# A four-layer recurrent block: w2 by chunk of the contraction in four column tiles, d and u folded, dense blocks read a slot later

## The chip, the cores and the metric

One core of a Trainium2 chip runs the kernel. The metric is device time in microseconds (us) of one execution; the host only lays data out.

## The reference

x is 32 sequences of 128 steps of 512 features, cond one row of 512 for each sequence. Four layers follow each other, each added to x:

```python
d = rsqrt(einsum('bi,io->bo', ys * ys, w0 * w0) + EPS)         # ys = cond / sqrt(512)
x1 = x + einsum('bsi,io->bso', x * ys[:, None], w0) * d[:, None]
h = tanh(h @ wh1 + x1_t @ wx1 + b1); x2_t = x1_t + h           # 128 steps, h0 = cond
xw = gelu(layernorm(cond) @ hw1 + hb1) @ hw2 + hb2             # 512 -> 2 * 512 * 8
layer = base + einsum('bdr,bkr->bdk', *halves(xw))             # rank 8, one for each sequence
x3 = x2 + (x2 + einsum('btc,bco->bto', x2, layer))
i, f, o, g = gates(x3_t @ wx3 + b3 + h @ wh3)                  # LSTM, 128 steps, h0 = cond
out_t = x3_t + o * tanh(f * c + i * g)
```

## The kernel before, in words

Time is cut into 32 tiles of 4 steps. Each large product is made in float16 with both operands split into a high and a low part (three products are summed); a scale, a power of two, comes from the largest magnitude of the operand. ScalarE makes the high part (`high`, L444), VectorE the low one (`low`, L625). Largest magnitudes go over the partitions by `partition_all_reduce` on GpSimd (`spread`, L391, for weights; L407 and L425 for tiles of x).

All five engines run lists written out by hand, joined by semaphores. The lists go by slots t = -13 to 127 (`SLOTS`). Slot t holds LSTM step t (from t = 0 on) and the step r of the tanh recurrence (RNN) that `slot_of` puts there: r = t + LEAD in the slots before 0, after that the remaining steps are spread over slots 0 to 117, so some slots (39, 78, 117 and all later ones) have none. a is the LSTM's tile, s = t % 4.

TensorE's slot: `gates_h` (L1120, 48 matmuls in four column tiles) waits for the split LSTM state; `gates_x` of the next step (L1112); `rnn_product` (L1129, L1132); the transpose of the LSTM state (L1175), which waits for VectorE's `lstm_h` (L904); behind it the dense work: by r % 4, halves of `l0` (layer 0's product of tile r//4 + 1) at 0 and 1 and of `l1` (x1 by wx1) at 2 and 3, and by s the layer 2 product `l2` of tile a + 1 (`z` and a quarter of base at s = 0, two quarters at 1, the last and the low rank part at 2). In the slots before t = 0 the w2 pieces of `W2_AFTER` come last.

VectorE's slot: gates out of PSUM (L894), the cell (L897 to L901), `lstm_h`, the RNN sums (L910, L913), the low parts of both states (L919, L928), then the pieces that prepare tiles: at s = 0 `mask_z`, `gate_scales`, `zm_low`; at r % 4 = 1 `x1` (layer 0's result out of PSUM) and `x1_low`; at s = 2 `x3` (layer 2's result); at r % 4 = 3 `tile_scales`, `xs_low` and `xw1` (layer 1's input part out of PSUM); `x2_low` at slots 4a - 5. ScalarE makes the high parts in the same slots. GpSimd adds x2 = x1 + h (L418) each step, ScalarE's tanh of step r waits for that of step r - 1; GpSimd also makes `xs` (x times ys, L399), one tile every four steps, and the partition reduces.

Before the slots lie the loads, the scales and splits of w0, wx1 and wh1, d (L997), the layer norm and u = ae by hw1 (L1004), `l0(0)`, w2 pieces 0 and 1, and `l1(0)`. In the slots before t = 0 also the wx3 and wh3 squares, scales and halves, base, and the layer 2 weights out of w2 are made. A w2 piece is one output chunk: a bias matmul (L1017) and four float32 matmuls (L1021) with 32 columns of weights, all into one column tile of the array; its megabyte comes by one DMA into a ring of four buffers. `copy_rows` moves four finished pieces to SBUF, `move_b` turns b, and after the last piece (t = -1) come `turn_a`, the reduce of a, and layer 2 of tile 0.

SP's list issues all loads in order, with the waits for free buffers between them.

## Time and profile before

| | us |
|---|---|
| median of 3 runs (1312.89 to 1316.41) | 1315.82 |
| the profiled execution | 1317.44 |
| its span, first to last instruction | 1315.4 |
| TensorE busy | 1239.2 (94%) |
| VectorE busy | 795.9 (61%) |
| ScalarE busy | 440.2 (33%) |
| GpSimd busy | 117.7 (9%) |
| TensorE clock granted, mean | 0.982 |

The profile is of one execution. PE is TensorE, PEld its weight loads, DVE VectorE, ACT ScalarE, POOL GpSimd, SP the queue that issues DMAs. Times are us from the first instruction. An instruction's line number is that of the code above; a name stands for a tile without its buffer's number, and several small tiles share storage (x1T, x2 in x_ring, zm and x3T in late). "[1.20 <-DVE lstm_h L904]" behind an instruction is the idle time of its engine before it and what ended it; "issue" is time in which the engine waited for nothing that the profile shows. A float32 matmul leaves two records. The granted clock is a share of 2.4 GHz.

### The profile page before, as it was taken

How to read it: one execution, taken by the hardware profiler on the slowest of the kernel's cores; microseconds unless marked ns; L12 is line 12 of the kernel's file. 1: busy time of each engine (PE TensorE's matmuls, PEld its weight loads, DVE VectorE, ACT ScalarE, POOL GpSimd, SP SyncE). 2: the span in 40 equal slices, each digit the busy share in tenths (PEclk: the TensorE clock that was granted, in tenths of full speed). 3: DMA queues.
4: the chain of work that ended last, by engine and by line, in shares of the span. 5: the costliest groups of instructions: out<-in, count | busy, mean ns of one | idle time of the engine just before them, and what ended most of it. 6: DMA issues, size and time to landing. Idle time of an engine off the chain costs nothing.

```text
span 1315.4 us, 50704 instructions
## 1 busy us (share of the span) xinstructions
PE 1239.2 (94%) x22900; PEld 793.1 (60%) x22900; DVE 795.9 (61%) x2235; ACT 440.2 (33%) x1110; POOL 117.7 (9%) x210
## 2 busy tenths in 40 slices
PE   6949979999999999999999999999999999999997
PEld 5433336666666666666666666666666666666553
DVE  5444546656666666656666666666666666665543
ACT  4253323232332333233333333333333333333322
POOL 2001101001000101000011011100100111000000
PEclk9978889999999999999999999999999999999999
DMA  9832300000000000000000000000000000000000
GB/s 327 335 130 98 112 9 12 17 19 18 19 18 13 17 19 12 17 19 18 19 16 13 19 19 19 19 19 19 18 11 19 19 11 11 11 11 11 10 10 18
DMA packets 22472, 50.99 MB, mean 39 GB/s; under 512 B 1920, under 2 KB 2048, under 8 KB 21232
## 3 DMA queue, kind: packets, MB, share of 16 engines
q1 hardware_dynamic: 22256, 47.75, 10.2%
q8 instruction: 179, 2.93, 0.9%
q14 instruction: 37, 0.30, 0.1%
HBM read 39.36 MB, written 8.39 MB: 36 GB/s over the span
## 4 chain that ended last, share of the span: by engine, by line
PE 73%; DVE 14%; ACT 6%; issue 5%; DMA 1%; SPq 0%; POOL 0%; DVEq 0%; POOLq 0%; ACTq 0%
PE ps_gates L1120 21%; PE ps_gates L1112 19%; PE ps_l L1054 12%; PE ps_x L1054 8%; PE ps_rnn L1129 4%; PE ps_rnn L1132 3%; PE ps_gates L1021 2%; PE ps_lstm_t L1175 2%; PE ps_z L1054 2%; DVE gates_ring L894 1%; ACT gates_ring L525 1%; PE ps_lstm_t L1021 1%; DVE xw1T L721 1%; ACT cell_tanh L530 1%; DVE lstm_h L904 1%
## 5 line engine op out<-in xcount | busy, mean ns | idle before, releaser
L1120 PE MATMUL ps_gates<-big,lstm_h 128*32 128x512 f16 x6144 | 356.7, 381 | 6.0 <-ACT lstm_h L444 6.0
L1112 PE MATMUL ps_gates<-big,rows 128*32 128x512 f16 x6144 | 353.7, 379 | 1.7 <-DVE rows L625 1.7
L1112 PEld LDWEIGHTS ps_gates<-big,rows 128*32 128x32 f16 x6144 | 164.6, 97 | 168.4 <-issue 1.7
L1120 PEld LDWEIGHTS ps_gates<-big,lstm_h 128*32 128x32 f16 x6144 | 153.1, 97 | 159.4 <-ACT lstm_h L444 8.4
L894 DVE SCALAR_TENSOR_TENSOR gates_ring<-ps_gates,tile_un,rows 128x256 f32<-128x256 f32 x256 | 111.9, 479 | 133.5 <-PE ps_gates L1120 133.5
L525 ACT ACTIVATE gates_ring<-gates_ring 128x256 f32<-128x256 f32 x128 | 53.3, 416 | 378.1 <-DVE gates_ring L894 378.1
L418 POOL TENSOR_TENSOR x_ring<-x1T,rnn_h 128x128 f32<-128x128 f32 x128 | 60.8, 475 | 899.2 <-ACT rnn_h L539 681.4
L1129 PEld LDWEIGHTS ps_rnn<-rnn_h,wh_hi 128*128 128x128 f16 x2048 | 90.8, 97 | 66.7 <-issue 56.4
L1129 PE MATMUL ps_rnn<-rnn_h,wh_hi 128*128 128x64 f16 x2048 | 121.3, 192 | 9.7 <-DVE rnn_h L928 9.7
L1132 PE MATMUL ps_rnn<-rnn_h,wh_lo 128*128 128x32 f16 x2048 | 116.5, 177 | 0.0
L928 DVE SCALAR_TENSOR_TENSOR rnn_h<-rnn_h,scales 128x128 f16<-128x128 f32 x128 | 76.3, 596 | 42.2 <-ACT rnn_h L444 39.5
L910 DVE SCALAR_TENSOR_TENSOR rnn_half<-ps_rnn,un_rnn,xw1T 128x128 f32<-128x128 f32 x128 | 44.8, 350 | 91.1 <-PE ps_rnn L1132 90.6
L444 ACT ACTIVATE lstm_h<-ps_lstm_t,tile_g 128x128 f16<-128x128 f32 x128 | 47.1, 368 | 149.0 <-PE ps_lstm_t L1175 149.0
L1132 PEld LDWEIGHTS ps_rnn<-rnn_h,wh_lo 128*128 128x128 f16 x2048 | 91.7, 97 | 0.0
L1054 PE MATMUL ps_l<-xs,w_hi 128*128 128x128 f16 x1024 | 81.5, 225 | 8.2 <-DVE xs L625 8.2
L1054 PE MATMUL ps_l<-x,wx_hi 128*128 128x128 f16 x1024 | 79.4, 221 | 6.9 <-DVE x L625 6.9
L1054 PE MATMUL ps_x<-x,base_hi 128*128 128x128 f16 x1024 | 79.4, 221 | 2.6 <-DVE base_lo L625 2.6
L1054 PEld LDWEIGHTS ps_l<-xs,w_hi 128*128 128x128 f16 x1024 | 68.8, 102 | 8.9 <-DVE xs L625 6.3
L904 DVE TENSOR_TENSOR lstm_h<-gates_ring,cell_tanh 128x128 f32<-128x128 f32 x128 | 38.3, 299 | 57.6 <-ACT cell_tanh L530 57.6
L1054 PEld LDWEIGHTS ps_l<-x,wx_hi 128*128 128x128 f16 x1024 | 67.5, 101 | 8.6 <-DVE x L625 7.2
L530 ACT ACTIVATE cell_tanh<-cell 128x128 f32<-128x128 f32 x128 | 39.6, 309 | 88.2 <-DVE cell L901 88.2
L897 DVE TENSOR_TENSOR late<-gates_ring,cell 128x128 f32<-128x128 f32 x128 | 37.5, 293 | 48.1 <-ACT gates_ring L527 48.1
(185 smaller groups left out, 1616.3 us busy)
## 6 DMA issues: line engine op xcount, KB each, us to landing
ring<-in_hw SPq DMA_DIRECT2D x16, 1024.0 KB, 7.2
xT_sb<-in_xT SPq DMA_DIRECT2D x32, 256.0 KB, 2.8
outT<-late SPq DMA_DIRECT2D x32, 256.0 KB, 2.0
big<-in_wx SPq DMA_DIRECT2D x5, 1024.0 KB, 9.8
big<-in_wh SPq DMA_DIRECT2D x5, 1024.0 KB, 18.5
big<-in_w SPq DMA_DIRECT2D x1, 1024.0 KB, 5.6
big<-in_hw SPq DMA_DIRECT2D x1, 1024.0 KB, 12.4
late<-in_base SPq DMA_DIRECT2D x1, 1024.0 KB, 15.4
```

Source lines behind the costliest of these rows:

```text
L418: nc.gpsimd.tensor_tensor(x2T[i % X2_RING][:, :, s], x1T[i % 2][:, :, s], rnn_h[:], ALU.add)\
L444: return nc.scalar.activation(out_, in_, ACT.Copy, scale=scale)
L525: nc.scalar.activation(gates[:, 0:2 * P], gates[:, 0:2 * P], ACT.Sigmoid).then_inc(gates_acted, 1)
L530: nc.scalar.activation(cell_tanh[:], cell[:], ACT.Tanh).then_inc(cell_tanh_ready, 1)
L894: nc.vector.scalar_tensor_tensor(gates[:, half], ps_gates[t % 2][:, half], tile_un[:, a, 0:1], b3_sb[:, half], ALU.mult, ALU.add).then_inc ...
L904: nc.vector.tensor_tensor(lstm_h[:], gates[:, 2 * P:3 * P], cell_tanh[:], ALU.mult)\
L928: nc.vector.scalar_tensor_tensor(rnn_h16[:, :, 1], rnn_h[:], s_h, rnn_h16[:, :, 0], ALU.mult, ALU.subtract).then_inc(rnn_lo_ready, 1)
L1054: last = nc.tensor.matmul(psum, w, x, start=(first and n == 0), stop=(final and n == len(triples) - 1))
L1112: nc.tensor.matmul(ps_gates[t % 2][B * j:B * j + B, :], x16[:, part, k, at:at + B], wx3_part(w_part, k)[:, GW * j:GW * j + GW], start=(n = ...
L1120: last = nc.tensor.matmul(ps_gates[t % 2][B * j:B * j + B, :], lstm_h16[:, part, k], wh3_part(w_part, k)[:, GW * j:GW * j + GW], start=Fal ...
L1129: nc.tensor.matmul(ps_rnn[:, at:at + 2 * B], wh1_hi[:, k, P * oc:P * oc + P], rnn_h16[:, k].rearrange("p h b -> p (h b)"), start=(k == 0), ...
L1132: last = nc.tensor.matmul(ps_rnn[:, at:at + B], wh1_lo[:, k, P * oc:P * oc + P], rnn_h16[:, k, 0], start=False, stop=(k == KC - 1))
```

## The change

- w2 comes by chunk of the contraction: a megabyte of the ring now holds, for one of four chunks k, four output chunks j. `w2_unit` multiplies them in four column tiles side by side; the four biases come with k = 0. Sixteen units, as there were sixteen pieces.
- d and u are made in four column tiles (`folded_parts`), copied to SBUF by VectorE, and the four parts are added by matmuls with a stack of identities, `fold` (`unfolded`).
- The weight scales come one by one, as do the reduces behind them; tile 0's scale comes before those of tiles 1 to 3. hw1 is loaded before wh1, base later.
- LEAD is 14. `slot_of` then leaves slots 29, 58, 88, 117 and later ones without an RNN step.
- `l0`'s halves are made at r % 4 = 3 (for the tile after) and 0, and read (`x1`) at 1; `l1`'s at 2 and 3, and `xw1` stands at the next 0, before the RNN sums. Layer 2 of a tile is made at s = 3, 0 and 1, `x2_low` at slots 4a - 6; `mask_z` and `x3` keep their slots. `xs_low` moves to 2, `tile_scales` to 0, `x_magnitude` and its reduce to 3, GpSimd's `xs` to 1.
- The squares of wx3 and wh3, their halves, base's preparation, `copy_rows` and `move_b` shift by about a slot.

```diff
-LEAD = 13
+LEAD = 14
...
             def load_w2(n):
-                sp.dma_start(ring[:, n % RING].rearrange("p (k n) -> p k n", k=KC),
-                             hw2[1 - n // RANK, n % RANK].rearrange(by_chunk, p=P)).then_inc(ld_ring[n % RING], 16)
+                q, k = n // KC, n % KC
+                sp.dma_start(ring[:, n % RING].rearrange("p (j n) -> p j n", j=RH),
+                             hw2[1 - q // 2, RH * (q % 2):RH * (q % 2 + 1), P * k:P * k + P].rearrange("j p n -> p j n"))\
+                  .then_inc(ld_ring[n % RING], 16)
...
             load_weight(wx1, WX1_SLOT, ld_wx1)
+            load_weight(hw1, W1_SLOT, ld_w1)
             load_weight(wh1, WH1_SLOT, ld_wh1)
-            load_weight(hw1, W1_SLOT, ld_w1)
...
-            for n in range(RING + 2, 2 * RANK):
+            for n in range(RING + 1, 4 * KC):
                 sp.wait_ge(w2_used, n - RING + 1)
                 load_w2(n)
+                if n == RING + 1:
+                    sp.dma_start(late[:].rearrange("p (k n) -> p k n", k=KC), base.rearrange(by_chunk, p=P)).then_inc(ld_base, 16)
...
             xs(0)
+            pool.wait_ge(sq_ready, 1)
+            pool.wait_ge(cond_max_ready, 1)
+            spread(slice(0, 2))
+            pool.wait_ge(m_ready, 1)
+            spread_x(0, 1)
+            pool.wait_ge(sq_ready, 2)
+            spread(slice(2, 3))
             pool.wait_ge(sq_ready, 3)
-            pool.wait_ge(cond_max_ready, 1)
-            spread(slice(0, 4))
+            spread(slice(3, 4))
             pool.wait_ge(m_ready, XT_RING)
-            nc.gpsimd.partition_all_reduce(m_all[:], m_part[:], P, MAX).then_inc(m_spread, XT_RING)
+            spread_x(1, XT_RING - 1)
             xs(1)
...
-                    if s == 2 and i + 2 < TILES:
+                    if s == 1 and i + 2 < TILES:
                         xs(i + 2)
-                    if s == 2 and XT_RING <= i + 3 < TILES:
+                    if s == 3 and XT_RING <= i + 3 < TILES:
                         pool.wait_ge(m_ready, i + 4)
                         wait(pool, tile_s_ready, i + 3)
-                        nc.gpsimd.partition_all_reduce(m_all[:, 0:1], m_part[:, 0:1], P, MAX).then_inc(m_spread, 1)
-                    if r == 2:
+                        spread_x(0, 1)
+                    if r == 3:
                         pool.wait_ge(sq_ready, 7)
-                        pool.wait_ge(base_max_ready, 1)
-                        spread(slice(7, 12))
+                        spread(slice(8, 12))
                     if r == 6:
                         pool.wait_ge(sq_ready, 11)
                         spread(slice(12, 16))
-                    if r == 9:
+                    if r == 10:
+                        pool.wait_ge(base_max_ready, 1)
                         pool.wait_ge(b_max_ready, 1)
                         spread(slice(4, 6))
+                        spread(slice(7, 8))
...
+            act.wait_ge(w_scale_ready, 1)
+            high(flat(w0_hi), big[:, W0_SLOT], s_w0).then_inc(w_hi_ready, 1)
+            act.wait_ge(d_var_ready, 1)
+            nc.scalar.activation(root_d, var_d, ACT.Sqrt).then_inc(d_root_ready, 1)
+            xs_high(0)
+            act.wait_ge(w_scale_ready, 2)
+            high(flat(wx1_hi), big[:, WX1_SLOT], s_wx1).then_inc(w_hi_ready, 1)
             act.wait_ge(ld_wh1, 16)
             act.wait_ge(sq_ready, 2)
             squares(unused16, big[:, WH1_SLOT], 3)
-            act.wait_ge(d_var_ready, 1)
-            nc.scalar.activation(root_d, var_d, ACT.Sqrt).then_inc(d_root_ready, 1)
-            act.wait_ge(scales_ready, 1)
-            high(flat(w0_hi), big[:, W0_SLOT], s_w0).then_inc(w_hi_ready, 1)
...
             nc.scalar.activation(hyperT, hyperT, ACT.Gelu).then_inc(hyper_ready, 1)
+            x1_high(0)
+            act.wait_ge(w_scale_ready, 3)
             high(flat(wh1_hi), big[:, WH1_SLOT], s_wh1).then_inc(w_hi_ready, 1)
+            act.wait_ge(h_scale_ready, 1)
             high(rnn_h16[:, :, 0], condT_sb[:], s_h).then_inc(h0_hi, 1)
-            x1_high(0)
-            act.wait_ge(xs_lo_ready, 1)
             xs_high(1)
...
+            WX3_SQUARED = {1: (0,), 2: (1, 2), 3: (3,)}
+            WH3_SQUARED = {4: (0,), 5: (1, 2), 6: (3,)}
...
-                if r is not None and r < KC:
-                    wx3_squares(r)
-                if r is not None and 3 <= r < 3 + KC:
-                    wx3_high(r - 3)
+                if r is not None and r in WX3_SQUARED:
+                    for k in WX3_SQUARED[r]:
+                        wx3_squares(k)
                 if r is not None and 4 <= r < 4 + KC:
-                    wh3_squares(r - 4)
-                if r == 7:
-                    copy_rows(1)
+                    wx3_high(r - 4)
...
-                if r is not None:
-                    c = r // STEPS + 1
-                    if r % STEPS == 1 and c < TILES:
-                        x1_high(c)
-                    if r % STEPS == 3 and c + 1 < TILES:
-                        wait(act, l0_ps, c + 1)
-                        xs_high(c + 1)
+                    x3_high(a + 1)
+                if t in x2_split and t != -1:
+                    x2_high(x2_split[t])
+                if r is not None and r % STEPS == 2 and r // STEPS + 2 < TILES:
+                    xs_high(r // STEPS + 2)
...
+
+            def weight_scale(n):
+                dve.wait_ge(absmax_spread, n)
+                col = slice(n, n + 1)
+                linked(nc.vector.tensor_scalar(exps[:, col], absmax_all[:, col], LEAST ** 2, None, ALU.max))
+                linked(exponents(exps[:, col], exps[:, col]))
+                half_exponents(exps[:, col])
+                over_power(scales[:, col], exps[:, col], TOP).then_inc(w_scale_ready, 1)
...
+            weight_scale(1)
+            linked(nc.vector.tensor_scalar(exps[:, 7:8], absmax_all[:, 0:1], 1.0, None, ALU.max))
+            linked(exponents(exps[:, 7:8], exps[:, 7:8]))
+            over_power(scales[:, 7:8], exps[:, 7:8], TOP).then_inc(h_scale_ready, 1)
+            dve.wait_ge(h_scale_ready, 1)
+            linked(nc.vector.tensor_scalar(m_shift[:, 0:1], s_h, 2.0 ** -(TOP - 3), None, ALU.mult))
+            dve.wait_ge(dsum_parts, 1)
+            nc.vector.tensor_copy(folded, ps_x3[:]).then_inc(dsum_moved, 1)
+            tile_scales(0, 1, 0)
+            dve.wait_ge(dsum_ready, 1)
+            nc.vector.tensor_scalar(var_d, ps_rnn[:, 0:P].rearrange("p (k b) -> p k b", b=B), L0_EPS, None, ALU.add)\
+              .then_inc(d_var_ready, 1)
+            weight_scale(2)
+            dve.wait_ge(w_scale_ready, 2)
+            tile_undo(0, 1, 0)
+            dve.wait_ge(u_parts, 1)
+            nc.vector.tensor_copy(folded, ps_z[:]).then_inc(u_moved, 1)
...
+            weight_scale(3)
+            dve.wait_ge(w_scale_ready, 3)
+            linked(nc.vector.tensor_tensor(un_rnn[:], s_wh1, s_h, ALU.mult))
+            linked(over_power(un_rnn[:], un_rnn[:], 0))
...
-            linked(over_power(un_rnn[:], un_rnn[:], 0))
+            for c in range(1, XT_RING):
+                x_magnitude(c, c)
+            tile_scales(1, XT_RING - 1, 1)
+            tile_undo(1, XT_RING - 1, 1)
             xs_low(1)
             dve.wait_ge(ld_b1, 16)
-            xw1(0)
...
                 if r is not None:
+                    if r % STEPS == 0:
+                        xw1(r // STEPS)
+                        dve.wait_ge(xw1_ready, r // STEPS + 1)
                     dve.wait_ge(rnn_ps, r + 1)
-                    dve.wait_ge(xw1_ready, r // STEPS + 1)
...
-                    if r == 1:
-                        linked(base_rows(0))
-                    if r == 2:
-                        base_magnitude()
-                    if r == 3:
+                    if r == 4:
                         wx3_scale()
...
-                    if r == 8:
-                        b_magnitude()
-                    if r == 10:
-                        b_bounds()
+                    if 5 <= r < 5 + KC:
+                        wx3_low(r - 5, 1)
                     if 9 <= r < 9 + KC:
                         wh3_low(r - 9, 1)
+                    if r == 8:
+                        base_diagonal()
+                        linked(base_rows(0))
+                    if r == 9:
+                        base_magnitude()
+                    if r == 10:
+                        b_magnitude()
+                    if r == 12:
+                        b_bounds()
+                c, ahead = (-1, -1) if r is None else (r // STEPS + 1, r % STEPS)
...
+                if ahead == 1 and c < TILES:
+                    x1(c)
...
-                        x1(c)
-                    if r % STEPS == 2 and XT_RING <= c + 2 < TILES:
-                        dve.wait_ge(m_spread, c + 2)
-                        x_magnitude(c + 2, 0)
+                if ahead == 3 and XT_RING <= c + 2 < TILES:
+                    x_magnitude(c + 2, 0)
+                if ahead == 0 and XT_RING <= c + 1 < TILES:
+                    tile_scales(c + 1, 1, 0)
+                    tile_undo(c + 1, 1, 0)
+                if ahead == 1 and c < TILES:
+                    x1_low(c)
...
-                if r is not None:
-                    c = r // STEPS + 1
-                    if r % STEPS == 1 and c < TILES:
-                        x1_low(c)
-                    if r % STEPS == 3:
-                        if XT_RING <= c + 2 < TILES:
-                            tile_scales(c + 2, 1)
-                        if c + 1 < TILES:
-                            xs_low(c + 1)
-                        if c < TILES:
-                            xw1(c)
+                if t in x2_split and t != -1:
+                    x2_low(x2_split[t])
+                if ahead == 2 and c + 1 < TILES:
+                    xs_low(c + 1)
...
+            def folded_parts(psum, xT_, w):
+                for k in range(KC):
+                    last = nc.tensor.matmul(psum[B * k:B * k + B, :], xT_[:, k], w[:, k], start=True, stop=True,
+                                            tile_position=(0, B * k))
+                return last
+
+
+            def unfolded(psum):
+                for k in range(KC):
+                    last = nc.tensor.matmul(psum[:, B * k:B * k + B], folded[:, P * k:P * k + P], fold[:], start=True, stop=True)
+                return last
+
             pe.wait_ge(ys_ready, 2)
             pe.wait_ge(sq_ready, 1)
-            for oc in range(KC):
-                for k in range(KC):
-                    last = nc.tensor.matmul(ps_x3[:, B * oc:B * oc + B], w0_sq[:, k, P * oc:P * oc + P], ysq[:, k],
-                                            start=(k == 0), stop=(k == KC - 1))
-            last.then_inc(dsum_ready, 1)
+            folded_parts(ps_x3, ysq, w0_sq).then_inc(dsum_parts, 1)
+            pe.wait_ge(dsum_moved, 1)
+            unfolded(ps_rnn).then_inc(dsum_ready, 1)
...
+            def w2_unit(n):
+                q, k = n // KC, n % KC
                 if n == 0:
                     pe.wait_ge(hyper_ready, 1)
                     pe.wait_ge(ld_b2, 16)
-                if n == 2 * RH:
+                if n == 2 * KC:
                     pe.wait_ge(rows_ready, 1)
-
-                at = RANK * (1 - q // 2) + RH * (q % 2) + j
-                nc.tensor.matmul(ps_rows[q][B * j:B * j + B, :], ident[0:2 * RANK, at:at + 1].broadcast_to([2 * RANK, B]), b2_sb,
-                                 start=True, stop=False, tile_position=(0, B * j))
+                if k == 0:
+
+                    for j in range(RH):
+                        at = RANK * (1 - q // 2) + RH * (q % 2) + j
+                        nc.tensor.matmul(ps_rows[q][B * j:B * j + B, :], ident[0:2 * RANK, at:at + 1].broadcast_to([2 * RANK, B]),
+                                         b2_sb, start=True, stop=False, tile_position=(0, B * j))
                 pe.wait_ge(ld_ring[n % RING], 16 * (n // RING + 1))
-                for k in range(KC):
-                    last = nc.tensor.matmul(ps_rows[q][B * j:B * j + B, :], hyperT[:, k], ring[:, n % RING, D * k:D * k + D],
+                for j in range(RH):
+                    last = nc.tensor.matmul(ps_rows[q][B * j:B * j + B, :], hyperT[:, k], ring[:, n % RING, D * j:D * j + D],
                                             start=False, stop=(k == KC - 1), tile_position=(0, B * j))
                 last.then_inc(w2_used, 1)
...
-            W2_AFTER = {0: (2, 3), 1: (4,), 3: (5,), 6: (6,), 7: (7,), 8: (8, 9), 9: (10,), 10: (11,), 11: (12, 13), 12: (14, 15)}
...
-            def l2(a, s):
-                if s == 0:
+            def l2(t):
+                s = t % STEPS
+                a = (t + 5) // STEPS
+                if a < TILES and (s == 3 or t == 0):
                     z(a)
                     wait(pe, x3_ready, a)
                     x3_base((0,))
-                if s == 1:
+                if a < TILES and s == 0:
                     x3_base((1, 2))
-                if s == 2:
+                if a < TILES and s == 1:
                     x3_base((3,))
                     x3_low_rank(a)
...
-            w2_piece(1)
+            w2_unit(0)
...
                 if r is not None:
-                    c = r // STEPS + 1
-                    if c < TILES:
-                        if r % STEPS == 0:
-                            l0(c, (0, 1))
-                        if r % STEPS == 1:
-                            l0(c, (2, 3)).then_inc(l0_ps, 1)
-                        if r % STEPS == 2:
-                            l1(c, (0, 1))
-                        if r % STEPS == 3:
-                            l1(c, (2, 3)).then_inc(xw1_ps, 1)
-                    if t >= 0 and a + 1 < TILES:
-                        l2(a + 1, s)
+                    c, ahead = r // STEPS + 1, r % STEPS
+                    if ahead == 0 and c < TILES:
+                        l0(c, range(KC) if c == 1 else (2, 3)).then_inc(l0_ps, 1)
+                    if ahead == 2 and c < TILES:
+                        l1(c, (0, 1))
+                    if ahead == 3 and c < TILES:
+                        l1(c, (2, 3)).then_inc(xw1_ps, 1)
+                    if ahead == 3 and c + 1 < TILES:
+                        l0(c + 1, (0, 1))
+                    if t >= 0:
+                        l2(t)
```

## Rows read from the trace of the kernel before

**Rows 1.** Stages: busy us (x instructions) of PE, PEld, DVE, ACT, POOL; clock; DMA.
```profile
45.00:176.00 131.00, 107.00 (x861) 48.05 (x857) 59.42 (x122) 47.92 (x63) 14.84 (x22) 0.87 0.40 151
...
920.00:1228.00 308.00, 308.00 (x6232) 204.90 (x6224) 197.69 (x575) 105.33 (x290) 27.27 (x49) 1.00 0.04 13
```

**Rows 2.** Waits of TensorE, 195 to 1316 us: total, times, longest.
```profile
PE ps_lstm_t L1175 <- DVE lstm_h L904: 22.0, 29, 2.9
PE ps_gates L1120 <- ACT lstm_h L444: 6.0, 13, 0.5
```

**Rows 3.** Timeline of TensorE: start, us, instruction, idle before and releaser.
```profile
198.60 0.31 PE L1175 MATMUL ps_lstm_t<-ident,lstm_h 128*128 128x128 f32 x1
...
201.55 2.77 PE L1120 MATMUL ps_gates<-big,lstm_h 128*32 128x512 f16 x48
...
208.23 0.33 PE L1175 MATMUL ps_lstm_t<-ident,lstm_h 128*128 128x128 f32 x1 [0.35 <-DVE lstm_h L904]
...
227.82 0.33 PE L1175 MATMUL ps_lstm_t<-ident,lstm_h 128*128 128x128 f32 x1 [1.20 <-DVE lstm_h L904]
...
560.82 0.33 PE L1175 MATMUL ps_lstm_t<-ident,lstm_h 128*128 128x128 f32 x1 [2.17 <-DVE lstm_h L904]
561.60 4.46 PE L1120 MATMUL ps_gates<-big,lstm_h 128*32 128x512 f16 x48 [0.46 <-ACT lstm_h L444]
```

**Rows 4.** Timeline of VectorE: h0_lo, r = 7, t = -1, t = 0.
```profile
37.87 0.35 DVE L625 SCALAR_TENSOR_TENSOR rnn_h<-condT_sb,scales,rnn_h 128x128 f16<-128x128 f32 x1
...
117.72 0.15 DVE L681 TENSOR_TENSOR m_exp<-m_all,m_least 128x3 f32<-128x3 f32 x1
...
118.91 0.75 DVE L625 SCALAR_TENSOR_TENSOR xs<-xsT,tile_s,xs 128x512 f16<-128x512 f32 x1
...
188.94 0.75 DVE L625 SCALAR_TENSOR_TENSOR rows<-ps_x,tile_un,rows 128x512 f16<-128x512 f32 x1 [3.98 <-ACT rows L444]
...
190.27 0.74 DVE L625 SCALAR_TENSOR_TENSOR x<-x_ring,tile_s,x 128x512 f16<-128x512 f32 x1
...
200.34 0.35 DVE L928 SCALAR_TENSOR_TENSOR rnn_h<-rnn_h,scales 128x128 f16<-128x128 f32 x1 [0.36 <-ACT rnn_h L444]
200.99 0.29 DVE L832 TENSOR_TENSOR late<-ps_z,same_b 128x128 f32<-128x128 f32 x1 [0.30 <-PE ps_z L1054]
...
202.18 0.28 DVE L705 TENSOR_SCALAR d_un<-dT,tile_s 128x128 f32<-128x128 f32 x1
...
204.70 0.75 DVE L625 SCALAR_TENSOR_TENSOR x<-x1T,tile_s,x 128x512 f16<-128x512 f32 x1 [0.79 <-ACT x L444]
```

**Rows 5.** Timeline of TensorE in the start: d, a w2 piece, b.
```profile
10.75 7.01 PE L997 MATMUL ps_x<-added,big 128*128 128x32 f32 x32 [1.02 <-ACT big L450]
...
51.03 1.04 PE L1017 MATMUL ps_gates<-x_ring,ident 16*32 16x512 f32 x2
52.00 3.62 PE L1021 MATMUL ps_gates<-ring,lstm_h 128*32 128x512 f32 x8
...
137.04 1.08 PE L1032 MATMUL ps_x<-rows,half_ident 128*64 128x512 f32 x4
```

**Rows 6.** Waits of GpSimd, whole span.
```profile
POOL x_ring L418 <- issue: 217.9, 30, 8.9
POOL m_all L425 <- issue: 166.4, 28, 6.3
```

**Rows 7.** Timeline of GpSimd.
```profile
175.66 0.38 POOL L391 PARTITION_ALL_REDUCE absmax_all<-absmax  x1 [10.20 <-DVE absmax L628]
```

**Rows 8.** Timeline of ScalarE.
```profile
46.13 0.31 ACT L539 ACTIVATE rnn_h<-rnn_pre 128x128 f32<-128x128 f32 x1 [10.61 <-DVE rnn_pre L913]
...
82.88 0.31 ACT L539 ACTIVATE rnn_h<-rnn_pre 128x128 f32<-128x128 f32 x1 [5.65 <-POOL x_ring L418]
...
105.79 1.89 ACT L450 ACTIVATE gates_ring<-big 128x2048 f16<-128x2048 f32 x1
```

**Rows 9.** Granted clock around slot 39, columns as in rows 1.
```profile
558.00:566.00 8.00, 5.37 (x65) 2.12 (x61) 3.21 (x10) 2.19 (x6) 0.10 (x1) 0.79 0.10 35
```

186 lines of the change are left out of this document (88 added, 98 removed).

## The prediction, made before the run

> **What bounds the kernel now.** I read the stage table first [rows 1]. From 45 to 176 us, the start in which the tanh recurrence runs alone, TensorE is busy for 107 of 131 us, and the granted clock is 0.87. In the main stage it has no gap at all in the third quarter (308.00 of 308). So the start can be shortened, and the main stage can hardly be: what is left there are stalls. The waits of TensorE after 195 us sum to 28.0 us [rows 2]; all are waits for the LSTM cell on VectorE (L904) or for its split (L444). The timeline shows their pattern [rows 3]: while tile boundary and RNN phase stand as they do before t = 39, two slots of each four stall the transpose L1175, by 0.35 us and by 1.20 us (ten and nine times); at t = 39, a slot without RNN step, the stall is 2.17 us, 0.46 us follow, and the next L1120 group takes 4.46 us in place of 2.77. That is 3.5 + 10.9 + 2.2 + 0.5 + 1.7 = 18.8 us, and some 1.4 us of single waits until t = 117: 20.2 us in all. The remaining 9.7 us lie in the last eleven slots, which the change leaves alone.
>
> **The rule of a stall.** VectorE comes late to the gates where its work at the end of a slot is longer than TensorE's. In slot 0 the transpose starts at 198.60 and the last piece on VectorE ends at 204.70 + 0.67 = 205.37, 6.77 us later; behind the transpose TensorE has 2.71 us of dense work D; the stall is 0.35 [rows 3, 4]. So stall = x - D - 3.71, with x the end of VectorE's work after the transpose. RNN split done is at x = 2.1 (200.34 + 0.35 - 198.60), so with E the work behind it, stall = E - D - 1.61. With D = 0, L1120 starts 0.78 us after the transpose (561.60 - 560.82) where otherwise D + 0.24 (201.55 - 198.60) pass: D counts as 0.54, and 0.5 us are lost at L1120 besides.
>
> **Main stage, added.** Prices [rows 4]: mask_z and gate_scales 1.0 with zm_low 1.2 (200.99 to 202.18), x1 1.75 and then 0.79 of waiting for ScalarE's half and 0.67 for x1_low (202.18 to 205.37), x3 1.33 (188.94 to 190.27), x2_low 0.67, xs_low 0.67, tile_scales with tile_undo 1.2 (117.72 to 118.91). xw1 now stands before the RNN sums, in time that VectorE has free once the cell is done: nothing, unless VectorE is late already. Moving l0, l1 and L2 a slot ahead removes VectorE's waits for TensorE. What stays is how the pieces meet, and slot_of sets that: with LEAD 14 the gaps are at t = 29, 58, 88, 117, and r % 4 = 0 falls on t % 4 = 2, 3, 0 and 1 in the four stretches between.
> First stretch, seven periods: s = 2 has E = 1.2 + 1.33 + 0.67 = 3.2 against D = 1.34, s = 3 has E = 3.2 against 1.38: 0.44 a period, 3.1 us.
> Second, seven: s = 0 carries mask, x1 and x1_low, 1.0 + 1.75 + 0.79 + 0.67 = 4.2, against D = 1.34: 1.24 each, 8.7 us.
> Third, seven: 0.24 each, 1.7 us.
> Fourth, from t = 90, six times: r % 4 = 1 meets s = 2. E = 1.75 + 0.79 + 0.67 + 1.33 + 0.67 = 5.2, and TensorE has nothing behind the transpose, since the list gives no l0 or l1 at r % 4 = 1 and no L2 at s = 2. Stall 5.2 - 0.54 - 1.61 = 3.1, with the 0.5 at L1120 3.6: 21.8 us, and 0.5 at t = 114.
> Gaps: 1.8 us together, mostly the 0.46 at L1120.
> Sum 37.6 us against 20.2: +17.4.
> **Moved out.** One RNN product (0.86 us) and half an l0 (1.34 us) go from the main stage to the start: -2.2.
> **Clock.** The 2.17 us stall was followed by a stretch at 1.2 in place of 2.4 GHz: 0.79 of the clock granted over 558 to 566 us [rows 9], 1.7 us lost in L1120. Six stalls of 3.1 us could cost 0 to 10.2 us; since one event in mid-kernel carries the price, I take the middle, 5.
>
> **The start, removed.** A w2 piece costs 3.55 + 0.97 us [rows 5], sixteen 72.3. A unit puts four column tiles side by side; the two half-width tiles of b show that float32 products overlap so, four records in 1.08 us where a lone pair takes 1.04. Sixteen units at 0.9 and four biases at 1.0 make 18.4: 53.9 us less on TensorE. The d and u products drop from 7.01 each to about 1.8 of parts, 0.74 of copy and 1.75 of folding, but on VectorE the copies and scales now stand ahead of weight_low(0), so I count no gain there. Behind it ScalarE's square of wh1 (2.1) and weight_scale(3) (1.0) have moved ahead of wh1's halves, with 0.3 of hand-over: h0_lo, which ended at 38.2 [rows 4], ends near 41.6.
> **The start, what takes its place: GpSimd.** Every time it goes from ordinary work to a partition reduce, 5.94 us pass (166.4 / 28), and back to ordinary work 7.26 (217.9 / 30) [rows 6], with nothing that the profile shows: a pair costs 5.94 + 0.38 + 7.26 = 13.6 us. ScalarE's tanh of step r waits for the x2 sum of step r - 1; the 5.65 us at 82.88 are such a wait [rows 8]. Before, pairs lie behind r = 2, 6 and 9, 10; after, behind r = 3, 6, 7, 10 and 11. Moreover x_magnitude(1 to 3) moved behind h0_lo, so the reduce over tiles 1 to 3 comes at 43.5 and xs(1) only after the way back:
> - 41.6 + 1.9 (magnitudes) + 0.4 + 7.3 + 1.3 (xs) + 1.4 (halves) + 0.9 (xw1) + 0.8: tanh of r = 0 at 55.6, before 46.13 [rows 8].
> - r = 1 to 3 hold x1(1), four squares of 2.1 (1.89 and a read) on ScalarE [rows 8], and xs_high: about 20, so the sum of r = 3 at 75.8.
> - pair: 89.4. Steps 5 and 6 with wx3 halves and wh3 squares, 12.8: 102.2.
> - two pairs and a sum, 27.6: 129.9. Steps 9 and 10, 9.6: 139.5.
> - two pairs, two reduces, a sum, 28.0: 167.5. Step 13 1.4, and 5.9 to the reduce of a: 174.8.
> Before, that reduce is at 175.66 [rows 7]; what follows it is the same. Gain 0.9 us. Bounds: if no pair were waited for, ScalarE and VectorE alone give some 25 us less; if DMA or the split of r = 0 slip, 8 us more.
> DMA: w2 moves the same bytes in the same sizes; a ring load has a slot or more, which GpSimd now stretches: nothing. If short slots came back, unit 13 or 14 would wait for its megabyte, some us.
>
> **Sum.** +17.4 - 2.2 + 5.0 - 0.9 = +19.3. The profiled execution took 1317.44 us (span 1315.4), 1.6 above the median 1315.82: 1336.7 there, 1335 as a median.
>
> **Rivals.**
> A, faster: GpSimd's changes aren't waited for (only a first use of a kind is dear, or the change overlaps with the wait for its operand). Then the 54 us count as far as VectorE and ScalarE let them: -25 + 17.4 - 2.2 = -9.8, 1306, down to 1296 with smaller stalls. It decides from about 17 us of gain in the start. For it: 53.9 us leave the busiest engine. Against it: the 58 changes of rows 6 average 5.9 and 7.3 us. 0.18. The Trainium skill, GPSIMD Engine Reference, section Instruction dispatch, puts a load of about 6 us on the first call to a freshly loaded kernel: read as once a kernel's life, it gives A's time; by rows 6 the 5.94 agrees in size, but comes at each change of kind.
> B, faster: the start as I have it, but the stalls of the last stretch are hidden: -0.9 - 2.2 + 17.4 - 21.8 = -7.5, 1308. Against it is D = 0 there. 0.07.
> C, slower still: the late r = 0 and ScalarE's squares push every pair, +8, and full clock loss, +5: 1348. 0.1.
> D, the tiles don't overlap in float32: units cost what pieces cost, slots from r = 8 grow as before; about 1341. Rows 5 speak against it. 0.02.
> Forecast 0.55; of the 0.08 left half is slower, half no change. Of A and B 0.03 end within 0.3% (4 us, about what a measurement of this kernel can tell from no change). So slower 0.55 + 0.12 + 0.04 = 0.71, same 0.07, faster 0.22. Low 1304 takes in most of A and B, high 1347 the sum at full clock loss and part of C.
>
> **What would show it.** Right: ScalarE waits for GpSimd at the tanh of r = 5, 9 and 13; VectorE waits for ScalarE's xs half at 44 to 54; L1175 stalls about 3 us every fourth slot from t = 91, and 1.2 in the second stretch; w2 groups of some 0.9 us. Wrong: gates of t = 0 ending before 185 us (195.0 now), or a last stretch without stalls.

## The result, and the profile after

| | before | after |
|---|---|---|
| median of the runs, us | 1315.59 (4 runs) | 1377.27 (4 runs, 1374.46 to 1382.52) |
| span of the profiled execution | 1315.4 | 1375.6 |
| gates of t = 0 begin on VectorE | 195.25 | 208.00 |
| last LSTM cell: `lstm_h` of t = 127 begins | 1311.21 | 1371.44 |
| TensorE busy | 1239.2 (94%) | 1192.1 (87%) |
| TensorE clock granted, mean | 0.982 | 0.955 |

The changed kernel takes 1.0477 times as long (95% interval 1.0442 to 1.0512), 61.7 us more. The forecast had the sign, but its 1335 was 42 us too low and its range ended at 1347. Of the 60.2 us between the spans, 12.8 lie before the gates of t = 0 and 47.5 between them and the last cell.

The stages of the changed kernel (columns as in rows 1):

```profile
45.00:176.00 131.00, 60.71 (x896) 41.77 (x896) 61.72 (x130) 48.49 (x63) 14.58 (x23) 0.72 0.44 167
920.00:1228.00 308.00, 283.81 (x5524) 184.48 (x5513) 180.96 (x522) 93.92 (x259) 26.62 (x46) 0.97 0.04 14
```

TensorE is busy for 60.71 of 131 us in the start, where it was busy for 107.00 [rows 1]: 46 us of its work have gone, and still the gates of t = 0 begin 12.8 us later. The granted clock of the stage is 0.72 in place of 0.87. From 920 to 1228 it now idles for 24 us; before it had no gap there. TensorE's waits from 195 us on, answering to rows 2:

```profile
PE ps_lstm_t L1240 <- DVE lstm_h L961: 37.5, 36, 2.9
PE ps_gates L1177 <- DVE rows L661: 21.9, 7, 3.6
PE ps_gates L1185 <- ACT lstm_h L469: 9.2, 20, 0.5
```

The waits at the transpose (22.0 before) and at `gates_h` (6.0) have grown, and a new one has appeared: `gates_x` (L1177) waits for x3's low half, `rows`, for 21.9 us in seven waits. One of these, 1.7 us, lies ahead of the gates of t = 0 and is there before too; the other six are in the last stretch.

**The main stage.** The timeline of TensorE (start, us, instruction, idle before) shows one stall of the second stretch, one of the third, and the pair that comes with each tile of the last:

```profile
513.69 0.33 PE L1240 MATMUL ps_lstm_t<-ident,lstm_h 128*128 128x128 f32 x1 [2.21 <-DVE lstm_h L961]
...
784.92 0.33 PE L1240 MATMUL ps_lstm_t<-ident,lstm_h 128*128 128x128 f32 x1 [1.21 <-DVE lstm_h L961]
...
1039.35 2.77 PE L1185 MATMUL ps_gates<-big,lstm_h 128*32 128x512 f16 x48 [0.46 <-ACT lstm_h L469]
1045.66 4.46 PE L1177 MATMUL ps_gates<-big,rows 128*32 128x512 f16 x48 [3.54 <-DVE rows L661]
```

The four stretches have periods (four slots, from one such stall to the next) of 36.5, 37.5, 36.5 and 41.1 us; less their stalls the second and third leave 35.3. In the last, 0.46 at `gates_h` and 3.54 at `gates_x` are lost, and the 48 matmuls behind the long wait take 4.46 us instead of 2.77. The granted clock of that stretch (columns as in rows 1) is 0.61, and it was 1.00 in the 3.60 us before:

```profile
1045.60:1050.00 4.40, 4.34 (x48) 1.64 (x48) 3.19 (x9) 1.21 (x4) 0.00 (x0) 0.61 0.01 3
```

The timeline of VectorE in that slot:

```profile
1040.32 1.45 DVE L987 SCALAR_TENSOR_TENSOR rnn_h<-rnn_h,scales 128x128 f16<-128x128 f32 x1 [0.35 <-ACT rnn_h L469]
1041.69 0.27 DVE L752 TENSOR_SCALAR d_un<-dT,tile_s 128x128 f32<-128x128 f32 x1
...
1044.20 0.75 DVE L661 SCALAR_TENSOR_TENSOR x<-x1T,tile_s,x 128x512 f16<-128x512 f32 x1 [0.79 <-ACT x L469]
1044.87 0.74 DVE L661 SCALAR_TENSOR_TENSOR rows<-ps_x,tile_un,rows 128x512 f16<-128x512 f32 x1
...
1046.19 0.74 DVE L661 SCALAR_TENSOR_TENSOR x<-x_ring,tile_s,x 128x512 f16<-128x512 f32 x1
1046.85 0.87 DVE L951 SCALAR_TENSOR_TENSOR gates_ring<-ps_gates,tile_un,rows 128x256 f32<-128x256 f32 x2
```

and of GpSimd:

```profile
1039.93 0.45 POOL L442 TENSOR_TENSOR x_ring<-x1T,rnn_h 128x128 f32<-128x128 f32 x1 [8.59 <-ACT rnn_h L587]
1040.34 1.28 POOL L417 TENSOR_TENSOR xsT<-xT_sb,ysT 128x512 f32<-128x512 f32 x1
```

The RNN's low half (L987) takes 1.45 us, where the same instruction took 0.35 in rows 4 at 200.34. It starts 0.02 us before GpSimd's 1.28 us of `xs`, and ends 0.15 us after it. From t = 0 on 26 of its 114 executions are that long, one in each tile that has an `xs`. The kernel before had them too, at r % 4 = 2; VectorE and GpSimd there:

```profile
209.63 1.44 DVE L928 SCALAR_TENSOR_TENSOR rnn_h<-rnn_h,scales 128x128 f16<-128x128 f32 x1
...
209.66 1.27 POOL L399 TENSOR_TENSOR xsT<-xT_sb,ysT 128x512 f32<-128x512 f32 x1
```

There VectorE then waited 2.33 us for the next gates, so the 1.1 us cost nothing. In the changed kernel's slot no such time is left: behind L987 stand x1 (from 1041.69), the wait for its high half, x1_low (1044.20), x3's low half (1044.87, for which `gates_x` waits) and x2_low (1046.19); the next gates begin at 1046.85.

**The start.** The timeline of ScalarE, tanh of r = 0, 5, 9 and 13:

```profile
60.93 0.31 ACT L587 ACTIVATE rnn_h<-rnn_pre 128x128 f32<-128x128 f32 x1 [2.32 <-DVE rnn_pre L972]
...
96.32 0.31 ACT L587 ACTIVATE rnn_h<-rnn_pre 128x128 f32<-128x128 f32 x1 [2.62 <-POOL x_ring L442]
...
140.15 0.31 ACT L587 ACTIVATE rnn_h<-rnn_pre 128x128 f32<-128x128 f32 x1 [11.22 <-POOL x_ring L442]
...
179.70 0.31 ACT L587 ACTIVATE rnn_h<-rnn_pre 128x128 f32<-128x128 f32 x1 [12.75 <-POOL x_ring L442]
```

and that of GpSimd: the reduce of tiles 1 to 3 and `xs` of tile 1, the pair behind r = 3, the second of the two pairs behind r = 6 and 7, and the reduce of a:

```profile
44.86 0.37 POOL L410 PARTITION_ALL_REDUCE m_all<-m_part  x1 [15.19 <-DVE m_part L668]
56.55 1.25 POOL L417 TENSOR_TENSOR xsT<-xT_sb,ysT 128x512 f32<-128x512 f32 x1 [11.32 <-issue]
...
88.26 0.39 POOL L405 PARTITION_ALL_REDUCE absmax_all<-absmax  x1 [6.71 <-issue]
95.79 0.44 POOL L442 TENSOR_TENSOR x_ring<-x1T,rnn_h 128x128 f32<-128x128 f32 x1 [7.14 <-issue]
...
131.73 0.38 POOL L410 PARTITION_ALL_REDUCE m_all<-m_part  x1 [7.88 <-issue]
139.62 0.44 POOL L442 TENSOR_TENSOR x_ring<-x1T,rnn_h 128x128 f32<-128x128 f32 x1 [7.51 <-issue]
...
187.77 0.38 POOL L405 PARTITION_ALL_REDUCE absmax_all<-absmax  x1 [6.01 <-issue]
```

Tanh of r = 0 comes at 60.93 (46.13 before [rows 8]), the reduce of a at 187.77 (175.66 before [rows 7]). The way back from the reduce at 44.86 to `xs` of tile 1 takes 11.32 us, in which TensorE does nothing, and behind it `l0` runs at half speed (1.03 us for eight matmuls, 0.61 at full clock). The timeline of TensorE shows that, and two w2 units, as cheap as was thought:

```profile
59.52 1.03 PE L1117 MATMUL ps_l<-xs,w_hi 128*128 128x128 f16 x8 [15.03 <-DVE xs L661]
...
64.12 1.93 PE L1084 MATMUL ps_gates<-ring,lstm_h 128*32 128x512 f32 x16
```

1.93 us for two units, 0.96 each (a lone one takes 1.06 to 1.08), where the matmuls of a piece took 3.62 [rows 5].

### The profile page after: what moved, and what is told of

Read it like the earlier page. It is cut to its first block, busy times and chain, and to the rows that moved or that the text cites. A ratio compares the mean times of both kernels' runs of the same rounds, so it can differ in the third digit from the quotient of the medians.

```text
span 1375.6 us, 50564 instructions
## 1 busy us (share of the span) xinstructions
PE 1192.1 (87%) x22868; PEld 778.9 (57%) x22868; DVE 793.7 (58%) x2252; ACT 436.9 (32%) x1110; POOL 118.3 (9%) x219
## 4 chain that ended last, share of the span: by engine, by line
PE 63%; DVE 17%; issue 11%; ACT 8%; DMA 1%; POOL 0%; SPq 0%; DVEq 0%; POOLq 0%; ACTq 0%
PE ps_gates L1185 18%; PE ps_gates L1177 18%; PE ps_l L1117 10%; PE ps_x L1117 6%; PE ps_rnn L1194 4%; PE ps_rnn L1197 2%; ACT x L469 2%; DVE x1T L759 2%; DVE x1T L755 2%; PE ps_lstm_t L1240 1%; DVE gates_ring L951 1%; PE ps_z L1117 1%; DVE rnn_h L987 1%; ACT rnn_h L469 1%; ACT gates_ring L573 1%
## 5 line engine op out<-in xcount | busy, mean ns | idle before, releaser
L1177 PE MATMUL ps_gates<-big,rows 128*32 128x512 f16 x6144 | 363.5, 387 | 21.9 <-DVE rows L661 21.9
L1177 PEld LDWEIGHTS ps_gates<-big,rows 128*32 128x32 f16 x6144 | 166.7, 98 | 196.6 <-DVE rows L661 24.7
L987 DVE SCALAR_TENSOR_TENSOR rnn_h<-rnn_h,scales 128x128 f16<-128x128 f32 x128 | 78.2, 611 | 54.5 <-ACT rnn_h L469 52.1
L1117 PEld LDWEIGHTS ps_l<-x,wx_hi 128*128 128x128 f16 x1024 | 68.7, 102 | 15.6 <-DVE x L661 13.6
L1240 PE MATMUL ps_lstm_t<-ident,lstm_h 128*128 128x128 f32 x128 | 40.1, 313 | 37.6 <-DVE lstm_h L961 37.5
## 6 DMA issues: line engine op xcount, KB each, us to landing
big<-in_hw SPq DMA_DIRECT2D x1, 1024.0 KB, 10.2
```

The source lines that it names most:

```text
L987: nc.vector.scalar_tensor_tensor(rnn_h16[:, :, 1], rnn_h[:], s_h, rnn_h16[:, :, 0], ALU.mult, ALU.subtract).then_inc(rnn_lo_ready, 1)
L1117: last = nc.tensor.matmul(psum, w, x, start=(first and n == 0), stop=(final and n == len(triples) - 1))
L1177: nc.tensor.matmul(ps_gates[t % 2][B * j:B * j + B, :], x16[:, part, k, at:at + B], wx3_part(w_part, k)[:, GW * j:GW * j + GW], start=(n = ...
L1240: nc.tensor.transpose(ps_lstm_t[:, 0:P], lstm_h[:], ident[:]).then_inc(lstm_t_ps, 1)
```

## The experiments

Thirteen kernels. The kernel before was timed again beside each group of them, at 1312.2 to 1315.0 us; the ratios given are to that time, and differences between kernels of different groups carry some 2 us of it. Line numbers in an experiment's rows are those of its own text, a few lines off from the changed kernel's where an edit takes lines out.

### The w2 units alone, on the kernel before

```diff
-                q, j = n // RH, n % RH
+                q, k = n // KC, n % KC
...
-                for k in range(KC):
-                    last = nc.tensor.matmul(ps_rows[q][B * j:B * j + B, :], hyperT[:, k], ring[:, n % RING, D * k:D * k + D],
+                for j in range(RH):
+                    last = nc.tensor.matmul(ps_rows[q][B * j:B * j + B, :], hyperT[:, k], ring[:, n % RING, D * j:D * j + D],
```

with the loads and the biases as in the change, and all else as before.

> The kernel before with w2 by chunk in four column tiles alone: 53.9 us of TensorE leave the start, nothing else moves. Theory G (GpSimd's changes between ordinary work and reduces set the start once TensorE doesn't): before, only the tanh of r = 4 and r = 8 waits for GpSimd, the other slots for TensorE; those shorten to about the 8 to 9 us of ScalarE's and VectorE's work, and two pairs of changes behind r = 6 and 9, 10 become the bound: 20 to 32 us less, 1284 to 1296. Rival T (TensorE's time is what the start costs, whoever else works): 45 us or more less, below 1272. Rival N (the gain was hidden anyway): within 5 us of 1315.

Measured: 1300.02 us, 0.989 of before (0.9861 to 0.9918). The gates of t = 0 begin at 177.76 instead of 195.25, and from there to the last cell it takes 1116.6 us (before 1116.0). This part of the change gives 14 to 17 us. The time lies 4 us above the range that theory G gave (1284 to 1296) and far from both rivals; T is refuted: some of the 54 us of TensorE's work were on the path, the rest stood beside ScalarE, VectorE and GpSimd.

### The changed kernel with the old w2 pieces

```diff
-                q, k = n // KC, n % KC
+                q, j = n // RH, n % RH
```

with the loads and matmuls of w2 as before, and all else as in the change.

> The changed kernel with w2 in pieces again, one column tile each, as before; everything else as changed. Theory G: the slots behind r = 3, 6, 7, 10 and 11 wait 13 to 15 us for GpSimd whatever TensorE does, so the 54 us of TensorE that come back lie mostly beside those waits: 2 to 12 us slower than the changed kernel (1379 to 1389). Rival T: 35 us or more slower.

Measured: 1390.24 us, 1.0581 (1.0555 to 1.0607), 13 us above the changed kernel and 1 us past the end of G's range; gates of t = 0 at 218.79, 10.8 us later, and the main stage as long as before (1163.6). The units are worth 11 to 13 us here too, and theory T falls for the second time. So the 61.7 us are a loss of some 75 by the other parts, less this gain.

### GpSimd's `xs` in another slot

```diff
-                    if s == 1 and i + 2 < TILES:
+                    if s == 0 and i + 2 < TILES:
                         xs(i + 2)
```

> The changed kernel with GpSimd's product xs at r % 4 = 0 in place of 1, one character. Theory P (VectorE's low part of the RNN state, L987, takes 1.45 us in place of 0.35 where GpSimd makes its sum and xs back to back, and that slot is the one that holds x1): the 1.45 moves to the slot of r % 4 = 0 or is spread there, stalls of the transpose fall from 0.85, 2.21 and 1.21 us to about 0, 1.2 and 0.2, and the last stretch loses 1.1 of 5.7 us a period: 20 to 30 us faster than the changed kernel, 1347 to 1357. Rival V (the 1.1 us too much in each stretch come from VectorE's own order, xw1 before the sums): no change of the stalls, within 4 us of 1377.

Measured: 1343.11 us, 1.0217 (1.0201 to 1.0234), 34 us below the changed kernel, more than expected; 30.5 of it from the first gates on and 3.6 ahead of them (of these 3.6 it isn't shown that they belong to the edit: three kernels with the same start, the changed one and two further down, have these gates at 205.42 to 208.00). VectorE's low half at L987 is back at 0.35 us, in all tiles of the main stage but one:

```profile
550.69 0.35 DVE L987 SCALAR_TENSOR_TENSOR rnn_h<-rnn_h,scales 128x128 f16<-128x128 f32 x1 [0.36 <-ACT rnn_h L469]
```

and GpSimd's `xs` runs elsewhere, behind a change of kind:

```profile
563.66 0.45 POOL L442 TENSOR_TENSOR x_ring<-x1T,rnn_h 128x128 f32<-128x128 f32 x1 [6.80 <-issue]
564.08 1.27 POOL L417 TENSOR_TENSOR xsT<-xT_sb,ysT 128x512 f32<-128x512 f32 x1
```

The stalls fall by 1.1 us in three stretches: 2.21 to 1.12 in the second, 1.21 to none in the third, 3.54 to 2.45 at `gates_x` in the last. In the first the 0.86 us of one slot vanish. That the instruction is slowed by GpSimd's `xs` beside it is shown by this run and by its converse further down (four edits).

### One recurrent step in every slot

```diff
-RNN_SPREAD = 118
+RNN_SPREAD = 114
```

> The changed kernel with RNN_SPREAD 114 in place of 118: no slot without an RNN step until 114, so r % 4 = 0 stays on t % 4 = 2 and the second, third and fourth stretch never come; the number of slots with and without RNN is the same. Theory S (what the main stage loses is set by how r % 4 and t % 4 meet): all 28 periods take 36.5 us as in the first stretch, none 37.5 or 41.1, no stall at gates_x but that of t = -1: 23 to 33 us faster than the changed kernel, 1344 to 1354. Rival O (the order of pieces costs its time in any phase, or the lone slots cost it): within 8 us of 1377.

Measured: 1342.09 us, 1.0208 (1.0190 to 1.0226), 35 us below the changed kernel. Nearly all periods are 36.5 us (the longest 36.9), and `gates_x` waits nowhere in the main stage. Theory S holds: the last stretch's cost is that x1 and x3 share a slot.

### x3 ahead of x1 where both share a slot

```diff
+                if t >= 0 and s == 2 and a + 1 < TILES:
+                    x3(a + 1)
                 if ahead == 1 and c < TILES:
                     x1(c)
...
                     x1_low(c)
-                if t >= 0 and s == 2 and a + 1 < TILES:
-                    x3(a + 1)
```

and x3's high part ahead of x1's on ScalarE.

> The changed kernel with x3 (both engines' parts) ahead of x1 and x1's halves in a slot that holds both. Theory X (in the last stretch gates_x waits 3.5 us for x3's low half because x1, the wait for its high half and its low half stand ahead of it on VectorE, and one half-clock stretch of 1.7 us follows): the six periods of the last stretch take 36.5 to 37.5 us instead of 41.1, the other stretches stay, time 1348 to 1358. Rival Z (x3 itself is ready too late, since z and the low-rank product come late on TensorE): the wait at gates_x stays above 2 us and the time above 1368.

Measured: 1384.04 us, 1.0528 (1.0504 to 1.0552), 7 us above the changed kernel (its interval ends at 1.0512), and as much from the first gates to the last cell. Both expectations failed: X in all, Z in the wait that it kept. The wait at `gates_x` is gone (0.36), but the transpose of the next slot waits as long:

```profile
1045.28 2.77 PE L1177 MATMUL ps_gates<-big,rows 128*32 128x512 f16 x48 [0.36 <-DVE rows L661]
...
1052.51 0.47 PE L1240 MATMUL ps_lstm_t<-ident,lstm_h 128*128 128x128 f32 x1 [3.49 <-DVE lstm_h L961]
```

The period of the last stretch is 41.3 us, against 41.1, and in the first stretch, where x3's slot had a stall of 0.2 to 0.5 us, it now has 0.5 to 1.0. So the order within the slot doesn't help: VectorE has more work in it than the slot holds, and TensorE waits for the rest at one place or at the other.

### Two pairs of changes fewer in the start

```diff
-                if ahead == 3 and XT_RING <= c + 2 < TILES:
+                if ahead == 2 and XT_RING <= c + 2 < TILES:
                     x_magnitude(c + 2, 0)
...
-                    if s == 3 and XT_RING <= i + 3 < TILES:
+                    if s == 2 and XT_RING <= i + 3 < TILES:
```

The first is VectorE's, the second GpSimd's.

> The changed kernel with the magnitude of the later x tiles, and its reduction on GpSimd, one slot earlier, so that in the start they stand right behind the reductions at r = 6 and r = 10 and two of the five pairs of changes of kind are gone. Theory G (in the start the path runs through GpSimd's changes of kind; the waits of tanh at r = 9 and r = 13, 11.2 and 12.8 us, are those of the two pairs that follow each other): both waits fall under 4 us, the reduction of a comes 12 to 24 us earlier (164 to 176 instead of 187.8), main loop unchanged within 4 us, time 1353 to 1366. Rival L (the start is held by the loads, the squares and the rounding of wx3 and wh3, GpSimd only stands beside it): the reduction of a comes less than 6 us earlier, time at least 1371.

Measured: 1362.72 us, 1.0368 (1.0342 to 1.0394), 14.6 us below the changed kernel; the reduce of a at 172.06, 15.7 us earlier, main loop 1163.0 us (1163.4 without the edit). GpSimd's timeline in this run:

```profile
117.62 0.38 POOL L410 PARTITION_ALL_REDUCE m_all<-m_part  x1 [5.71 <-issue]
117.92 0.90 POOL L405 PARTITION_ALL_REDUCE absmax_all<-absmax  x1
```

and ScalarE's tanh of r = 9 and 13:

```profile
133.04 0.31 ACT L587 ACTIVATE rnn_h<-rnn_pre 128x128 f32<-128x128 f32 x1 [1.97 <-DVE rnn_pre L972]
...
164.33 0.31 ACT L587 ACTIVATE rnn_h<-rnn_pre 128x128 f32<-128x128 f32 x1 [3.96 <-DVE rnn_pre L972]
```

The two reduces stand back to back, with nothing between them, and neither tanh waits for GpSimd any more. Theory G holds: a change of kind (GpSimd going from ordinary work to a reduce or back) is paid for each change, not for each reduce.

### The magnitudes of tiles 1 to 3 early

```diff
+            pool.wait_ge(m_ready, XT_RING)
+            spread_x(1, XT_RING - 1)
             pool.wait_ge(sq_ready, 3)
             spread(slice(3, 4))
-            pool.wait_ge(m_ready, XT_RING)
-            spread_x(1, XT_RING - 1)
...
+            for c in range(1, XT_RING):
+                x_magnitude(c, c)
             weight_low(0, w0_lo, w0_hi, W0_SLOT, s_w0)
...
-            for c in range(1, XT_RING):
-                x_magnitude(c, c)
```

> The changed kernel with the magnitudes of x tiles 1 to 3 taken on VectorE ahead of the low half of w0 and reduced on GpSimd ahead of the last weight column, so that the product ysT times x of tile 1 follows the third reduction instead of the fourth. Theory E (the first recurrent step waits 12 to 15 us for the change back to tensor_tensor behind the late reduction at 44.86): tanh of r = 0 comes at 46 to 52 us instead of 60.9, reduction of a 8 to 14 us earlier, time 1362 to 1369. Rival W (the next thing is late as well: w2 units, wx3 loads, so the gain is eaten by the rest of the start): tanh of r = 0 comes early but the reduction of a by under 4 us, time at least 1372.

Measured: 1367.15 us, 1.0398 (1.0367 to 1.0428), 10.1 us below the changed kernel. Tanh of r = 0 comes at 49.66, 11.3 us earlier; the gates of t = 0 8.1 us earlier. GpSimd's timeline at the last early reduce and `xs` of tile 1:

```profile
31.02 0.74 POOL L405 PARTITION_ALL_REDUCE absmax_all<-absmax  x1
38.44 1.26 POOL L417 TENSOR_TENSOR xsT<-xT_sb,ysT 128x512 f32<-128x512 f32 x1 [6.68 <-DVE x1T L759]
```

Theory E holds.

### The two edits of the main stage together

```diff
-RNN_SPREAD = 118
+RNN_SPREAD = 114
...
-                    if s == 1 and i + 2 < TILES:
+                    if s == 0 and i + 2 < TILES:
```

> The changed kernel with both earlier edits, ysT times x in the slots of r mod 4 = 0 and a spread of 114 (one recurrent step in each slot until they end). Each alone gave 34 to 35 us. Theory P plus S (two separate causes, VectorE's slowed instruction beside GpSimd in all stretches and the phase at which x1 and x3 meet in the last): periods of 35.4 to 35.8 everywhere, time 1306 to 1318. Rival O (one and the same cause, both edits only move x1 away from x3): time 1334 to 1345.

Measured: 1321.90 us, 1.0059 (1.0036 to 1.0081). That is 4 us above the range of P plus S, and 12 below that of O. Added, the gains would be 69 us; they are 55: some 10 are counted twice in the second, third and last stretch, by their periods, and 4 ahead of the first gates. From the first gates to the last cell it takes 1110.0 us, in place of 1163.4: 53.5 of the changed kernel's main stage are these two causes, and what is left is 6 us shorter than before.

### d's and u's products as before

```diff
-            folded_parts(ps_x3, ysq, w0_sq).then_inc(dsum_parts, 1)
-            pe.wait_ge(dsum_moved, 1)
-            unfolded(ps_rnn).then_inc(dsum_ready, 1)
+            product(ps_rnn, ysq, w0_sq).then_inc(dsum_ready, 1)
```

`product` is the loop of four by four matmuls of before; u likewise, and VectorE's two copies go.

> The changed kernel with d's and u's products as before (sixteen matmuls each, no parts, no copy, no folding). Theory N (the fold gains nothing: TensorE has nothing else to do there, and VectorE's two copies and two waits, some 3 us, stand ahead of everything that follows): the low half of xs of tile 0 ends 2 to 4 us before 29.4, time 1370 to 1377. Rival F (the fold is what makes the start of the changed kernel as early as it is): time 1380 to 1387, 5 us per product later.

Measured: 1373.88 us, 1.0442 (1.0414 to 1.0470), 3.4 us below the changed kernel, and the gates of t = 0 3.7 us earlier. The intervals overlap, so the traces have to decide. TensorE's timeline of this run, d's and u's products:

```profile
10.79 7.01 PE L1044 MATMUL ps_rnn<-added,big 128*128 128x32 f32 x32 [1.06 <-ACT big L475]
17.61 7.01 PE L1044 MATMUL ps_l<-cell_tanh,big 128*128 128x32 f32 x32
```

VectorE's, the low half of tile 0's xs:

```profile
25.23 0.74 DVE L661 SCALAR_TENSOR_TENSOR xs<-xsT,tile_s,xs 128x512 f16<-128x512 f32 x1
```

The changed kernel's, `unfolded` of d on TensorE:

```profile
21.94 1.91 PE L1054 MATMUL ps_rnn<-fold,x1T 128*128 128x32 f32 x8 [9.05 <-DVE x1T L730]
```

and the same low half on VectorE:

```profile
28.72 0.74 DVE L661 SCALAR_TENSOR_TENSOR xs<-xsT,tile_s,xs 128x512 f16<-128x512 f32 x1
```

The two products take 7.01 us each but are done at 24.6; folded, d's takes 1.93 and 1.91 us and waits 9.05 between them for VectorE's copy. The low half comes 3.5 us earlier without the fold, and tanh of r = 0 at 56.91, where it lies at 59.78 to 62.43 in the seven kernels that have the fold and late magnitudes. In time the fold costs about 3 to 4 us: 3.4 here, 4.4 in the pair of kernels in the next section, whose intervals don't overlap. Theory N holds.

### Four edits, five edits

Early magnitudes, later magnitudes a slot earlier, `xs` at r % 4 = 0 and the spread of 114:

> The changed kernel with all four edits: magnitudes of x tiles 1 to 3 early, later magnitudes one slot earlier, ysT times x in slots of r mod 4 = 0, spread 114. If the four causes are separate, the gains add: 1321.9 less 10.1 (early) less 14.5 (later magnitudes) = 1297, expected 1290 to 1303, faster than before by 1 to 1.8 per cent. If the two edits of the start overlap (the waits that one takes away are those that the other shortens), 1304 to 1312. The run says nothing for the change as made; it asks whether the causes found account for the loss.

and with d and u as before on top:

> The same, and d's and u's products as before. Theory N: 1 to 4 us below the run with the four edits. Rival F: 3 to 10 us above it. The faster of the two is to be compared with the kernel before that had the w2 units alone, 1300.0.

Measured: 1316.33 us, 1.0008 (0.9994 to 1.0022), and 1311.96 us, 0.9978 (0.9964 to 0.9993). The first is 19 us above the expected 1297 and outside both ranges; the second is 4.4 us below the first, 0.4 more than theory N allowed. The start gave all it should (gates of t = 0 at 178.97 and 178.75), but the main loop takes 1129.7 and 1129.2 us instead of 1110.0. The first of the two, GpSimd:

```profile
204.67 0.45 POOL L442 TENSOR_TENSOR x_ring<-x1T,rnn_h 128x128 f32<-128x128 f32 x1 [6.70 <-ACT rnn_h L587]
205.08 1.29 POOL L417 TENSOR_TENSOR xsT<-xT_sb,ysT 128x512 f32<-128x512 f32 x1
```

VectorE in the same slot:

```profile
205.06 1.46 DVE L987 SCALAR_TENSOR_TENSOR rnn_h<-rnn_h,scales 128x128 f16<-128x128 f32 x1 [0.36 <-ACT rnn_h L469]
```

TensorE in the next:

```profile
208.44 2.77 PE L1177 MATMUL ps_gates<-big,rows 128*32 128x512 f16 x48 [0.83 <-DVE rows L661]
```

and GpSimd in the run with the two edits of the main stage:

```profile
592.62 0.44 POOL L442 TENSOR_TENSOR x_ring<-x1T,rnn_h 128x128 f32<-128x128 f32 x1 [7.05 <-issue]
593.04 1.73 POOL L417 TENSOR_TENSOR xsT<-xT_sb,ysT 128x512 f32<-128x512 f32 x1
```

There the reduce at r % 4 = 3 held GpSimd for 7.05 us of changing back, so that the sum and `xs` of the next slot came late, behind L987. With the reduce a slot earlier GpSimd is ready in time, `xs` starts beside L987 again, which takes 1.46 us, and x3 behind it comes 0.83 us late for `gates_x`. From t = 0 on L987 is slow in 26 tiles here and in none of the run with the two edits. Saving a pair of changes in the start brought the slowed instruction back in the main loop.

### The later magnitudes earlier in the start only

On top of the five edits:

```diff
-                if ahead == 2 and XT_RING <= c + 2 < TILES:
+                if ahead == (2 if t < 0 else 3) and XT_RING <= c + 2 < TILES:
```

and likewise on GpSimd.

> As the run with five edits (1312.0), but the later magnitudes are one slot earlier only while the recurrence runs alone (t below 0), and where they were from t = 0 on. Theory M (the magnitude in the slots r mod 4 = 2, where x3 and x2's low half stand at this spread, is what made the main loop 19 us longer, 1128 us against 1109 from the first gates to the last cell, by 0.8 us at gates_x and 0.3 at the transpose in each period): the start stays (gates of t = 0 at 180), the main loop takes 1107 to 1112 us, time 1291 to 1297, below the kernel before with the w2 units alone (1300.0). Rival R (an earlier start shifts something else, a load or the end of the recurrence): main loop above 1120, time 1303 to 1312.

Measured: 1291.78 us, 0.9842 (0.9827 to 0.9857), gates of t = 0 at 177.66, main loop 1108.8 us. The time is the one expected; the reason that theory M gave was half right. The edit is the right one, but at this spread x3 shares its slot with r % 4 = 0 and not with the magnitude; by the rows above, read later, it is the reduce's place on GpSimd that counts, and here the low half of the RNN state is slow in no tile of the main loop. This is the fastest version, 1.6% below the kernel before. It is 0.5% below the units alone by the ratios (0.984 against 0.989; the intervals, up to 0.9857 and from 0.9861, just don't overlap).

### The flat spread on the kernel before

```diff
-RNN_SPREAD = 118
+RNN_SPREAD = 115
```

> The kernel before with the w2 units and a spread of 115, one recurrent step in each slot. Theory P (what a spread costs or gives is set by which pieces share a slot: here x1 and mask_z share one in the first stretch, 0.35 and 1.20 us a period, and the third stretch has no stall; one phase for all keeps that of the first): 28 periods with 1.55 us in place of the mixture, time 1313 to 1328, 13 to 28 us slower than the 1300.0 without this edit, where the same edit took 35 us off the changed kernel. Rival Q (slots without a recurrent step cost something by themselves, so a flat spread helps every version): time below 1298.

Measured: 1327.28 us, 1.0124 (1.0102 to 1.0145), 27 us above the 1300.0 without the edit. TensorE late in the main stage:

```profile
930.36 0.33 PE L1179 MATMUL ps_lstm_t<-ident,lstm_h 128*128 128x128 f32 x1 [0.35 <-DVE lstm_h L906]
...
949.97 0.33 PE L1179 MATMUL ps_lstm_t<-ident,lstm_h 128*128 128x128 f32 x1 [1.21 <-DVE lstm_h L906]
```

These are the 0.35 and 1.20 us of rows 3, now in each period to the end of the recurrence. The same edit took 35 us off the changed kernel: a spread has no price of its own, it only says which pieces meet. Theory P holds.

## Why the prediction was right or wrong

The sign came out, the size didn't: by the spans 41 us are missing, 27.3 behind the gates of t = 0 and 13.7 ahead of them. Two steps failed. In the main stage, the work E of VectorE behind the transpose took the RNN split as done at x = 2.1, with its low half at 0.35 us; GpSimd's `xs`, moved beside it, was put at nothing and makes it 1.45 once a tile, some 19 us. In the start, the path was right and three of its terms were too small: the way back behind the reduce of tiles 1 to 3 (11.3 us for 7.3), the two double pairs with the sums around them (5.3 us more), and the `xs` of r = 13, left out.

**The w2 units.** Right in price (0.96 against 0.9). That "units cost what pieces cost" (rival D) is out. What failed is the bookkeeping: their gain was never separated from the rest of the start, and it is 11 to 17 us.

**The start, -0.9 forecast, +12.8 measured.** The path was named rightly: tanh of r = 5, 9 and 13 wait for GpSimd by 2.6, 11.2 and 12.8 us [rows 8 had 5.65 for one], and VectorE waits for xs's half in 44 to 54, in fact until 58.7. The sizes failed step by step. "Tanh of r = 0 at 55.6" was 60.93: the reduce came at 44.86 and not at 43.5, and the way back took 11.32 us and not the 7.3 that is the mean of rows 6. The steps of r = 1 to 3 were right (81.1 against 75.8 with the delay of 5.3). "Two pairs and a sum, 27.6" took 30.2 (from 109.95 to 140.15), "two pairs, two reduces, a sum, 28.0" 29.4 (from 150.28 to 179.70), the sums of r = 6 and 10 ahead of them took 0.6 more each than their siblings (1.08 and 1.09 us), and the `xs` of r = 13 (1.3) before the last reduce was left out: another 6.5 us. The fold, "no gain there", is a loss: without it tanh of r = 0 came at 56.91, some 4 us earlier. "The price of a pair, 13.6" is right for one alone (14.2 behind r = 3) and small for two in a row.

**"If no pair were waited for, 25 us less."** Two pairs taken out gave 16.5 at the gates of t = 0, and with the early magnitudes 26.8 (178.97 against 205.76). Of the same order as the bound, though changes behind r = 3, 6 and 10 are still there.

**Main stage, +17.4 forecast for the stalls.** The rule stall = E - D - 1.61 is right in the first three stretches once the slow instruction is gone: with `xs` at r % 4 = 0 they stall by mostly 0.2 to 0.5, 1.1 and 0 us, for 0.44, 1.24 and 0.24. Its E left out one term: `xs` moved on GpSimd from r % 4 = 2 to 1, where it stands beside the RNN's low half in the very slot that holds x1. The slowed instruction was in the trace of before, at r % 4 = 2, but in a slot with time to spare, and I priced GpSimd's move at nothing. So the periods of the first stretch are 36.5 us for the forecast's 35.7, the stalls of the second 2.21 for 1.24, of the third 1.21 for 0.24: some 19 us over 21 periods. The forecast's stall of the last stretch, 3.6 a period, was measured as 4.0 (0.46 and 3.54; 2.9 in the sixth), 23.0 in all for 21.8, though at another instruction: `gates_x`, not the transpose, because the low half of x3 is wanted there. That it came so near is in part luck: without the slow instruction this stretch stalls by 2.9 (0.46 and 2.45), so the 3.6 was 0.7 too much by itself, and the 1.1 that E lacked made up for it. As the run with x3 first shows, the place doesn't lower the price.

**Clock, +5 forecast.** The price of one event, 1.7 us, is right, and it came each time: 4.46 us instead of 2.77 in five tiles and 4.07 in the sixth, 9.8 us, where the middle between 0 and 10.2 was taken. These 4.8 and the 19 and 1.2 above are 25 of the 27 us that the main stage took beyond the forecast; the rest I haven't found.

**Moved out, -2.2.** Not visible by itself; the main loop of the fastest version takes 1108.8 us against 1116.0, and these 7 us hold it together with less stalling.

**The rivals.** A (1306: GpSimd's changes not waited for) is refuted by the run with two pairs fewer; B by the 21.9 us at L1177. C, slower by a late r = 0, was the nearest, and lacked the 19 us of the slowed instruction too. The Trainium skill, GPSIMD Engine Reference, section Instruction dispatch, says that the first call to a freshly loaded kernel pays about 6 us. The two reduces at 117.62 and 117.92 agree with it if each change of kind counts as a fresh load, which no run here shows by itself. The way back, for which the page has no figure, is longer here (6.7 to 11.3).

## What to carry to other kernels

When one engine's step is moved to another slot, price what runs beside it there: the same 1.3 us of GpSimd work cost nothing in one slot and 0.8 to 1.1 us in each period in the next, and an instruction whose duration in the trace differs from its siblings (1.44 at 65.06 us of the kernel before and then once in each tile, 0.35 in most other slots) is the sign to look for. Add up an engine's work in each slot for each phase in which the loops can meet; reordering inside a full slot only moved the wait. A part that saves time on the busiest engine should be timed alone: here one part gave 11 to 17 us and the rest hid it under 75.

## What the runs showed of the hardware

- VectorE's 128x128 scalar_tensor_tensor with two operands in SBUF takes 0.35 us, and 1.44 to 1.46 when it starts together with GpSimd's 128x512 tensor_tensor (1.27 to 1.29); the two then end within 0.15 us of each other. Where GpSimd's starts among VectorE's others it can be the one that is late: 1.73 at 593.04. The Trainium skill, SBUF — State Buffer, section Terms, says that the two engines share a port pair that one holds for a whole instruction while the other is blocked; the 1.45 agrees, and the profile shows the blocked time as a longer instruction and not as a wait.
- GpSimd's change from ordinary work to a reduce and back costs 5.7 to 7.9 and 6.7 to 8.0 us in the slots of the changed kernel, again at every change (58 of them in rows 6), and nothing between two reduces. One way back took 11.32 us (at the same place 10.8 to 11.3 in the other kernels with late magnitudes); the DMA engines were full then (share 1.02 from 45 to 56 us). In the run with early magnitudes it took 6.7 at a share of 0.19 (the profile names VectorE's x1T as what ended it, for which `xs` doesn't wait in the program). But before, 7.52 passed at a share of 1.05 (20 to 30 us), so DMA load alone doesn't explain it; this stays open.
- The half clock behind a wait doesn't follow from the wait's length alone. All six waits at `gates_x` in the last stretch (five of 3.54 to 3.57 us, one of 2.46) were followed by it. Of the seven of 2.21 to 2.56 at the transpose in the second, the first was: `l1`'s eight matmuls behind it took 0.98 and 1.06 us, and 0.61 behind the other six. In the run with `xs` at r % 4 = 0 six waits at `gates_x`, all of 2.45 or 2.46 us, were followed by 4.46, 2.77, 4.46, 4.15, 2.77 and 4.22 us for the same 48 matmuls. What tells these apart was not tried.
